# Two-layer Mamba and attention kernel: the sum y taken as tokens by channels through transposing passes, with another order of side work and softplus in PSUM

## The reference, cut to what matters

```
u  = silu(conv(xn @ Win_u) + convb);  z = xn @ Win_z          # 256 channels each
dt = softplus(dtr @ Wdt + bdt);  A = -exp(Alog)               # 16 states
h  = exp(dt_t * A) * h + (dt_t * u_t) * B_t                   # for every token, channel, state
y_t = sum over the 16 states of h * C_t
out = ((y + u * D) * silu(z)) @ Wout
```

## Time and profile before

| | us |
|---|---|
| median of 3 runs | 904.17 (902.27 to 907.8) |
| the profiled execution | 910.72 |
| its span, first to last instruction | 908.9 |
| scan stage, from the first scan to the last `finish` | 130.6 to 609.2 of the span |

### The profile page before, as it was taken

The page is one execution under the profiler, slowest core; times in us unless marked ns, Lnnn a source line. Parts: engine busy times, 40 slices in busy tenths (PEclk is TensorE's granted clock), DMA queues, the critical chain, the costliest instruction groups (busy, mean ns, idle before and its releaser), DMA issues.

```text
span 908.9 us, 10020 instructions
## 1 busy us (share of the span) xinstructions
PE 735.2 (81%) x2952; PEld 367.6 (40%) x2952; DVE 662.7 (73%) x957; ACT 468.6 (52%) x738; POOL 458.2 (50%) x392
## 2 busy tenths in 40 slices
PE   2879877788797896987978968667989788888886
PEld 1767732233242342432423323136776233334433
DVE  7574569999999899998999999984333454555543
ACT  2325646546466365474663654421353666676664
POOL 5120069898897988989889889922000000000000
PEclk9999989899898898997989979975889999999999
DMA  3422424444443443444444449400020000000000
GB/s 102 140 71 93 166 58 157 135 151 142 139 151 129 144 146 129 160 135 142 146 125 157 150 125 278 145 1 0 24 70 1 1 1 1 1 1 1 13 12 24
DMA packets 48118, 85.60 MB, mean 94 GB/s; under 512 B 6320, under 2 KB 11448, under 8 KB 48064
## 3 DMA queue, kind: packets, MB, share of 16 engines
q1 hardware_dynamic: 48064, 84.96, 29.2%
HBM read 83.37 MB, written 1.57 MB: 93 GB/s over the span
## 4 chain that ended last, share of the span: by engine, by line
DVE 33%; PE 27%; issue 21%; ACT 9%; POOL 7%; DVEq 1%; DMA 0%; POOLq 0%; ACTq 0%
DVE ps L832 11%; DVE hc L842 7%; DVE moe L832 6%; POOL drive L488 4%; PE ps L1309 3%; PE ps L1509 2%; PE ps L1478 2%; PE ps L1294 2%; ACT ps L625 2%; PE ps L1486 2%; POOL hc L496 2%; PE ps L1517 2%; PE ps L1422 2%; PE ps L1432 1%; DVEq L388 1%
## 5 line engine op out<-in xcount | busy, mean ns | idle before, releaser
L1260 PE MATMUL ps<-hc,ident 128*128 128x512 f32 x512 | 272.7, 661 | 80.0 <-POOL hc L496 50.6
L488 POOL TENSOR_TENSOR drive<-dtu,b_sb 128x512 f32<-128x512 f32 x256 | 321.5, 1277 | 28.7 <-DVE ps L832 13.3
L625 ACT ACTIVATE ps<-dt,negA 128x510 f32<-128x510 f32 x256 | 171.6, 685 | 163.1 <-DVE ps L832 120.3
L832 DVE TENSOR_TENSOR_SCAN ps<-ps,drive 128x512 f32<-128x512 f32 x193 | 230.7, 1222 | 30.2 <-ACT ps L625 17.9
L1260 PEld LDWEIGHTS ps<-hc,ident 128*128 128x128 f32 x512 | 97.9, 207 | 243.3 <-issue 86.0
L842 DVE TENSOR_TENSOR hc<-ps,c_sb 128x512 f32<-128x512 f32 x193 | 129.3, 670 | 0.0
L734 ACT ACTIVATE probs<-ps 128x1024 f32<-128x1024 f32 (+1 forms) x96 | 88.0, 917 | 77.3 <-PE ps L1486 67.0
L548 POOL TENSOR_TENSOR stat<-stat,halfc 128x4 f32<-128x4 f32 x8 | 8.1, 1007 | 223.5 <-DVE stat L1025 223.5
L496 POOL TENSOR_TENSOR hc<-moe,c_sb 128x512 f32<-128x512 f32 x63 | 80.3, 1275 | 1.7 <-DVE moe L832 1.7
L832 DVE TENSOR_TENSOR_SCAN moe<-ps,drive 128x512 f32<-128x512 f32 x63 | 76.2, 1209 | 0.0
L1509 PE MATMUL ps<-probs,v_ring 128*32 128x512 f32 x320 | 46.2, 651 | 0.0
(11 more groups left out here) (215 smaller groups left out, 994.4 us busy)
## 6 DMA issues: line engine op xcount, KB each, us to landing
b_sb<-bc_rows SPq DMA_DIRECT2D x128, 256.0 KB, 3.6
c_sb<-bc_rows SPq DMA_DIRECT2D x128, 256.0 KB, 3.3
wbuf<-in_pack SPq DMA_DIRECT2D x16, 514.0 KB, 3.3
wbuf<-in_pack SPq DMA_DIRECT2D x8, 512.0 KB, 4.4
x_sb<-in_x SPq DMA_DIRECT2D x4, 256.0 KB, 3.7
out<-x_sb SPq DMA_DIRECT2D x4, 256.0 KB, 2.3
w_in<-in_w_in SPq DMA_DIRECT2D x1, 512.0 KB
bc_rows<-bcx SPq DMA_DIRECT2D x8, 64.0 KB, 2.9
```

The costliest lines, as they stand in the source:

```text
L488: pool.tensor_tensor(drive[:, 2 * (N % DRIVES) + half], dtu[:, N // STATES % 2, half], b_sb[:, N % B_RING], ALU.mult) \
L625: act.activation(seqs(decay_bank(q))[:, :, lo:lo + SEQ - 1], seqs(dt[:, g % 2, half])[:, :, lo:lo + SEQ - 1], ACT.Exp, scale=negA[:, g // ...
L832: dve.tensor_tensor_scan(h_of(q)[:, turn], decay_bank(q)[:, turn], drive[:, 2 * (N % DRIVES) + half, turn], 0.0, ALU.mult, ALU.add).then_i ...
L1260: pe.matmul(ps[:, Y_BANK + half], ident[:], hc[:, 2 * (N % DEEP) + half], start=False, stop=True, skip_group_check=True).then_inc(sem["y_a ...
```

## The change

- y is summed as tokens by channels. `add_y` now has four instructions a half step: a block of 128 tokens of hc is stationary, the identity moves (128 columns) and the matmul is marked as a transpose that accumulates. u * D and the projection z are turned in the same way, four blocks each.
- yg is then tokens by channels, so a new event `y` turns it back once a group and half: PE transposes four blocks into the side bank (`turn_y`), ACT copies them to `yT` (`copy_y`), which lies in an unused part of `moe`, and `finish` uses yT.
- `LAG` is 3 and `DEEP` 5. In READERS each u stands one state later where a state follows it. POOL's half steps are the second halves of even states instead of odd ones, and its product with C stands between its two drives of a state.
- Softplus in PSUM: Relu is written back into the side bank, and DVE's sum reads it there and frees the bank; dt_b is gone. The semaphore dt_ready is replaced by side_free.

```diff
--- before.py
+++ after.py
@@ -48,8 +48,8 @@
...
 OWN_H = 2
-DEEP = 4
-LAG = 2
+DEEP = 5
+LAG = 3
@@ -80,7 +80,7 @@
...
     "taps_diag", "u_ready", "z_ready",
-    "dt_abs", "dt_exp", "dt_ln", "dt_ready", "dtu_ready",
+    "dt_abs", "dt_relu", "dt_exp", "dt_ln", "dtu_ready",
@@ -140,7 +140,7 @@
...
         if g:
-            slots[7] = ("finish", g - 1)
+            slots.update({3: ("y", g - 1, 0), 4: ("y", g - 1, 1), 7: ("finish", g - 1)})
@@ -148,9 +148,12 @@
...
             order.append(("state", g * STATES + j))
-    order += [("end",)] + [("finish", STEPS - 1)] + events("T20 T21 T22 T23")
+    order += [("end",), ("y", STEPS - 1, 0), ("y", STEPS - 1, 1), ("finish", STEPS - 1)] + events("T20 T21 T22 T23")
...
     rest = order[start:]
+    for k in reversed(range(len(rest) - 1)):
+        if rest[k][0] == "u" and rest[k + 1][0] == "state":
+            rest[k], rest[k + 1] = rest[k + 1], rest[k]
@@ -159,7 +162,7 @@
...
     last = rest.index(("end",))
-    rest[last:] = events("A20 S20 A21 S21") + [("end",)] + events("A22 B20 C20 S22 B21 C21") + \
+    rest[last:] = events("A20 S20 A21 S21") + [("end",), ("y", STEPS - 1, 0), ("y", STEPS - 1, 1)] + events("A22 B20 C20 S22 B21 C21") + \
@@ -167,7 +170,7 @@
...
          for kind in "ASBCT"}
-SIDE = {ev: n for n, ev in enumerate(ev for ev in ORDER if ev[0] in ("gate", "w", "u", "z", "x", "dt", "finish"))}
+SIDE = {ev: n for n, ev in enumerate(ev for ev in ORDER if ev[0] in ("gate", "w", "u", "z", "x", "dt", "y", "finish"))}
@@ -231,7 +234,7 @@
...
     N, half = divmod(q, HALVES)
-    return half == 1 and N % 2 == 1 and N < ALL - 1
+    return half == 1 and N % 2 == 0
@@ -288,7 +291,6 @@
...
         dt_a = sb("dt_a", [P, COLS])
-        dt_b = sb("dt_b", [P, COLS])
@@ -308,6 +310,7 @@
...
 
+        yT = moe[:].rearrange("p t d -> p (t d)")[:, 2 * COLS:4 * COLS].rearrange("p (n c) -> p n c", n=HALVES)
@@ -480,13 +483,11 @@
...
 
-            def drive_state(N):
-
-                for half in range(HALVES):
-                    pool.wait_ge(sem[f"b_loaded{N % B_RING}"], 16 * (N // B_RING + 1))
-                    after(pool, "scan_done", 2 * (N - DRIVES) + half + 1)
-                    pool.tensor_tensor(drive[:, 2 * (N % DRIVES) + half], dtu[:, N // STATES % 2, half], b_sb[:, N % B_RING], ALU.mult) \
-                        .then_inc(sem["drive_ready"], 1)
+            def drive_half(N, half):
+                pool.wait_ge(sem[f"b_loaded{N % B_RING}"], 16 * (N // B_RING + 1))
+                after(pool, "scan_done", 2 * (N - DRIVES) + half + 1)
+                pool.tensor_tensor(drive[:, 2 * (N % DRIVES) + half], dtu[:, N // STATES % 2, half], b_sb[:, N % B_RING], ALU.mult) \
+                    .then_inc(sem["drive_ready"], 1)
@@ -515,18 +516,21 @@
...
                         for first in range(DRIVES - 1):
-                            drive_state(first)
+                            for half in range(HALVES):
+                                drive_half(first, half)
...
                             pool.wait_ge(sem["dtu_ready"], HALVES * (M // STATES + 1))
-                        drive_state(M)
+                        drive_half(M, 0)
...
                         times_c(N - 1, 1)
+                    if M < ALL:
+                        drive_half(M, 1)
...
                     n = HALVES * g + half
-                    pool.wait_ge(sem["dt_ready"], n + 1)
+                    pool.wait_ge(sem["side_free"], SIDE[ev] + 1)
@@ -599,20 +603,27 @@
...
                         act.preload_act_table_set("natural_log_exp_and_others")
-                    after(act, "dt_ready", n)
                     act.activation(dt_a[:], side, ACT.Abs, bias=bias).then_inc(sem["dt_abs"], 1)
-                    act.activation(dt_b[:], side, ACT.Relu, bias=bias).then_inc(sem["side_free"], 1)
                     act.wait_ge(sem["dt_abs"], n + 1)
+                    act.activation(side, side, ACT.Relu, bias=bias).then_inc(sem["dt_relu"], 1)
...
 
+            def copy_y(ev):
+                _, g, half = ev
+                act.wait_ge(sem["e0_added"], PAIRS0)
+                act.wait_ge(sem["side_ready"], SIDE[ev] + 1)
+                if g:
+                    act.wait_ge(sem["side_ready"], SIDE["finish", g - 1] + 1)
+                act.activation(yT[:, half], side, ACT.Copy).then_inc(sem["side_free"], 1)
+
...
                 if j == 0:
-                    act.wait_ge(sem["dt_ready"], HALVES * (g + 1))
+                    act.wait_ge(sem["side_free"], SIDE["dt", g, HALVES - 1] + 1)
@@ -636,6 +647,8 @@
...
                     side_part(ev)
+                elif ev[0] == "y":
+                    copy_y(ev)
@@ -818,7 +831,8 @@
...
                     after(dve, "decay_ready", STATES * HALVES * (g - 1))
-                    dve.tensor_tensor(dt[:, g % 2, half], dt_a[:], dt_b[:], ALU.add).then_inc(sem["dt_ready"], 1)
+                    dve.wait_ge(sem["dt_relu"], HALVES * g + half + 1)
+                    dve.tensor_tensor(dt[:, g % 2, half], dt_a[:], side, ALU.add).then_inc(sem["side_free"], 1)
@@ -868,7 +882,7 @@
...
                     if g:
-                        dve.wait_ge(sem["side_ready"], SIDE["finish", g - 1] + 1)
+                        dve.wait_ge(sem["side_ready"], SIDE["y", g - 1, half] + 1)
@@ -1229,7 +1243,9 @@
...
                     pe.wait_ge(sem["ln_copied"], STAGE["T"]["T", 1, g % PAIRS] + 1)
-                    last = pe.matmul(side, w_in[:, dr, c:c + P], xmT[:, toks], start=True, stop=True)
+                    for t in range(4):
+                        tile = slice(toks.start + t * P, toks.start + (t + 1) * P)
+                        last = pe.matmul(side[:, t * P:(t + 1) * P], xmT[:, tile], w_in[:, dr, c:c + P], start=True, stop=True)
@@ -1250,15 +1266,29 @@
...
                     for half in range(HALVES):
-                        pe.matmul(ps[:, Y_BANK + half], diagD[:, g // PAIRS, half], u_s[:, g % 2, half],
-                                  start=True, stop=True, skip_group_check=True)
+                        for t in range(4):
+                            block = slice(t * P, (t + 1) * P)
+                            pe.matmul(ps[:, Y_BANK + half, block], u_s[:, g % 2, half, block], diagD[:, g // PAIRS, half],
+                                      start=(t == 0), stop=True, skip_group_check=True)
...
                         pe.wait_ge(sem["hc_ready"], own_before(2 * N + half + 1))
-                    pe.matmul(ps[:, Y_BANK + half], ident[:], hc[:, 2 * (N % DEEP) + half], start=False, stop=True,
-                              skip_group_check=True).then_inc(sem["y_added"], 1)
+                    for t in range(4):
+                        block = slice(t * P, (t + 1) * P)
+                        last = pe.matmul(ps[:, Y_BANK + half, block], hc[:, 2 * (N % DEEP) + half, block], ident[:],
+                                         start=False, stop=True, is_transpose=True, skip_group_check=True)
+                    last.then_inc(sem["y_added"], 1)
+
+            def turn_y(ev):
+
+                _, g, half = ev
+                side_free(ev)
+                pe.wait_ge(sem["gated"], HALVES * g + half + 1)
+                for t in range(4):
+                    last = pe.transpose(side[:, t * P:(t + 1) * P], yg[:, half, t * P:(t + 1) * P], ident[:])
+                last.then_inc(sem["side_ready"], 1)
@@ -1266,7 +1296,7 @@
...
                     for half in range(HALVES):
-                        last = pe.matmul(side[:, t * D:(t + 1) * D], yg[:, half, t * P:(t + 1) * P],
+                        last = pe.matmul(side[:, t * D:(t + 1) * D], yT[:, half, t * P:(t + 1) * P],
@@ -1325,6 +1355,8 @@
...
                     project(ev)
+                elif ev[0] == "y":
+                    turn_y(ev)
```

## The result

The changed kernel takes 897.35 us (median of 8 runs, 895.44 to 897.88); the kernel before, measured beside it, 909.84 (8 runs, 902.27 to 911.77). The ratio is 0.9864, 95% interval 0.9837 to 0.9892; the forecast was 0.9887, and 894 us in a range of 884 to 915. The 894 stood on a median before of 904.17 from three runs; on 909.84 the same ratio is 899.6. The kernel before is itself spread over 1% from one execution to the next, the changed one over 0.3%, and each profile is of one execution.

What follows compares the result with a forecast made beforehand. DVE's queue bounds the scan stage, busy 446.4 of 478.6 us with 17.9 waiting for ACT's decays. Terms -12.4 - 6.7 + 5.2 + 1.5 + 2.1 = -10.3 gave 900.4 profiled, 894 on the median; range 884 to 915.

Steps and rivals of the forecast that it cites:

- The order of u: At a group's start: ACT reads the first u after four decays, not two, removing DVE's waits there, -12.4 us.
- Softplus: DVE's sum for dt takes 670 ns with one operand in PSUM, against a mean of 1147: -6.7 us.
- rival 4: DVE's sum for dt is no cheaper, slowed by something other than two SBUF operands: 900.5 us; chance 0.12.
- The second dt matmul: On PE, it waits until DVE's sum frees the side bank; margin about 1.3 us, costed at nothing.
- The turns: Turning yg back: low PE clock in some two groups of three makes DVE's decays late, 7 x 0.75 = 5.2 us.
- Silu: At the Silu block: decay 1.0 us late instead of 0.79, +1.5 us over seven groups; the old 5.5 stay.
- The end: Last group's finish: turns and copies in series take 3.4 us, beginning 1.35 earlier; DVE waits there, +2.1 us.
- Y passes: PE's work on y falls from 1.7 to 1.0 us a state, priced at nothing since DVE does not wait for it.
- A sign of being wrong that came: The prediction is wrong if ACT's reads of z or x wait for a late PE by over a microsecond.
- rival 1: PE's clock holds in the scan stage: the 5.2 and 1.5 vanish, the end costs 1; -18, 886 us; chance 0.22.
- Rival 2: PE at half clock through the turns in every group: DVE waits 33 us against 17.9; 915 us; chance 0.17.
- Rival 3: PE saturates as transposing passes don't keep its clock up: about 8 us a group late, +33, 937 us; chance 0.07.

Runs made afterwards that it cites:

- e1: The kernel before with only softplus in PSUM added: 897.54 us, ratio 0.9899, stage 470.1 us.
- e5: The kernel before with softplus in PSUM and u read one state later, LAG 2, DEEP 4: 891.70 us, ratio 0.9838, stage 462.6 us.
- e3: The changed kernel without the y part (y summed as before; softplus and all orders kept): 904.72 us, ratio 0.9963, stage 477.9 us.
- e8: The changed kernel with additions of y as plain two-pass matmuls on the same blocks, without is_transpose: 913.75 us, ratio 1.0076, stage 485.4 us.
- e9: e5 with POOL's halves and order as in the changed kernel: 893.29 us, ratio 0.9835, stage 466.7 us.
- the four stages above: Stages with POOL's changed order: y as before 466.7 (LAG 2, e9) and 477.9 (LAG 3, e3); y part 473.3 (LAG 2) and 470.5 (LAG 3, changed).

## Why the prediction was right, and where it was not

The total lies inside the measured interval, and each wait of my sum is found in the changed kernel at its place and near its size. What failed is the account of what each part of the change is worth: two steps that I had priced at nothing are off by about 15 us each, in opposite directions, and they cancel. That is luck.

- **The order of u, -12.4.** Nothing of it is left at the first u; behind the second u 0.46 us stand in one group. Right as a place. It was not free: the change's orders hold LAG 3, whose effect on yg I did not follow. The move of u alone takes 7.5 us off the stage (470.1 in e1, 462.6 in e5), of waits for u that were 10.5 in e1.
- **Softplus, -6.7.** 14 sums at 674 ns against 1147: -6.6. Right, and rival 4 (no cheaper) is out. e1's stage fell by 8.5. The second dt matmul, costed at nothing, shows no wait of DVE.
- **The turns, +5.2.** 6.6 measured: 1.19, 0.82, 0.90, 0.75, 0.95, 0.83 and 1.13. The mechanism as I told it, u * D at half clock after PE's idle time; the price was too low because the low clock came in all seven groups (0.54 to 0.64 over u * D), not in two of three.
- **Silu, +1.5 on 5.5.** 8.3 in all against 7.0: 0.79 in the group without turns, 1.25 in the six others.
- **The end, +2.1.** +2.04.
- **Y passes "worth nothing by itself, since DVE does not wait for it".** This step failed. It was read off the kernel before, where PE had slack at z. In the changed order PE's way from yg to z is what ACT and so DVE wait for: without the short passes the stage is 7.4 us longer (e3), with two passes to each block 15.0 (e8). The total came out since I had also costed LAG 3 at nothing. Part by part, each put on top of the one before (e1, e5, e9, e3, changed), forecast and measured stage are: softplus -6.7 and -8.5; u -12.4 and -7.5; POOL's order 0 and +4.1; LAG 3 with DEEP 5 0 and +11.2; the y part +8.8 (5.2 + 1.5 + 2.1) and -7.4. The sums are -10.3 and -8.1. In another order the same parts have other prices, as the four stages above show.
- **Layer 1, not foreseen.** -5.95 us in unchanged code. With the terms up to `finish` alone (forecast -10.3, measured -7.15) the kernel would have come to about 0.992. So this too is luck in the agreement of 0.9864 with 0.9887.
- **A sign of being wrong that came.** I had said that the prediction is wrong if ACT's read of x waits for PE by over a microsecond. It does, by 1.97 us in six groups, and DVE loses nothing by it, so the sign was badly chosen. The others did not come: DVE does not wait for drives, and the transposes take one pass.

The rivals: the clock did not hold (0.78, forecast near 0.8), so rival 1 is out. Rival 2's low clock and its waits came in their places, but 15.3 in sum and not 33. Rival 3 is out: the stage got shorter, and PE did not run at half clock throughout. The row that I had held against it says less than I took from it, since the stretch right behind the two that I named, 648.27 to 651.68, was granted 0.50. The rise to 1.00 behind a stretch of nothing but accumulating transposes, in each of seven groups, decides it against that rival's premise. The Trainium skill, in TensorE: Matmul & The Clock Gate, Part 4: PE-mode transpose, has transposes not count as busy for the clock; the trace does not agree, for these f32 transposes. So the fall from 0.91 (e8) to 0.78 with the same blocks marked as transposes does not need that rule. It goes with an addition's eight blocks streaming for 1.04 instead of 1.95 us at full clock; that this is the whole cause is not shown.

## What to carry to other kernels

"The engine isn't waited for" holds for one order of the work: when a change also moves who comes when, follow each first instruction of a group (here yg, u * D, z) through every queue again before giving a faster step the price of nothing. Take a bundle apart before keeping it: here the cheapest piece with one three-line move gave 0.984 (0.978 with a second move), against 0.986 for the whole. The 0.984 and the 0.986 can't be told apart by their intervals, but the stage of the piece is 7.9 us shorter, with far less code. And an engine that reaches a wait earlier may leave it slower, if its clock falls while it stands there.
